# A graph-attention and mixture-of-experts kernel: where TensorE reads the addresses of a batch

## The chip, the cores and the metric

The kernel runs on one core of a Trainium2 chip. The metric is the device time of one launch, in microseconds (us), from the first to the last instruction of the program with what lies around them; lower is better. The engines of the core are named as in the profile: PE is TensorE's matmul, PEld its weight load, DVE is VectorE, ACT is ScalarE, POOL is GpSimd, SP is SyncE. A "q" behind a name (PEldq, ACTq) is the sequencer of that engine: the part that runs register and wait instructions and hands the others to the engine.

## The reference, cut to what matters

x has 6250 rows of 256, src and dst list 100000 edges sorted by dst.

```python
def _L0_gnn_ref(x, edge_index, W, attn, W_out):
    h = jnp.einsum('ni,hid->nhd', x, W)                  # 4 heads of 64
    e = jnp.einsum('ehd,hd->eh', h[src], a_src) + jnp.einsum('ehd,hd->eh', h[dst], a_dst)
    e = jnp.where(e > 0, e, 0.2 * e)
    alpha = jnp.exp(jnp.minimum(e - segment_max(e, dst)[dst], 20.0))
    alpha_norm = alpha / (segment_sum(alpha, dst)[dst] + 1e-08)
    return segment_sum(alpha_norm[:, :, None] * h[src], dst).reshape(N, 256) @ W_out

x = x + _L0_gnn_ref(_layernorm(x), edge_index, ...)
x = x + _L0_ffn_ref(_layernorm(x)[None], ...)[0]         # 8 experts, top 2, 256 -> 256 -> 256
```

## The kernel before, in words

A first part (lines 96 to 568) makes a table of h and its scores per node, and cuts the edges into tiles of 128, so that each tile's edges fall in one block of 125 destination nodes. The second part does everything else and is the part that the change touches. Its unit is a **batch** of 16 tiles; there are 52 batches.

**Iterations and slots.** Every engine has the same loop, `for it in range(-1, LAST)`, with 16 slots `k` in each iteration (lines 1282 to 1293 for TensorE). In iteration `it` TensorE sums the messages of batch `it`, one tile in each slot (`aggregate`, line 1113, 128x260 products into a PSUM bank), and works out the attention scores of batch `it + 1` in the same slots: the destination's part of the score of every edge (`d_of_edges`, line 1073, sixteen small products, called here D: eight in slot 0, D0, and eight in slot 1, D1), then the products of `chain` in slots 3, 5, 7 and 9 (lines 1081 to 1093), between which VectorE has its steps. VectorE starts on a batch's scores when D1 has ended (semaphore D), and line 1081 needs what VectorE makes of them (`eC`, line 794).

**The other stream.** From iteration 4 on the finished blocks of nodes go through the output projection, the layer norm, the router and the experts (`products`, lines 1137, 1183, 1189, 1214, 1240, 1249): three iterations for three blocks, 48 steps `s = s0 + k` with s0 = 0, 16 or 32 in turn. In slots whose s is in `FIRST = (0, 16, 25, 32)` these products stand ahead of the tile's aggregate, otherwise behind it; those of s = 18 stand in the slot of s = 17. With s0 = 0 slot 1 holds the second layer of an expert and the transposes of the router's weights (line 1240), with s0 = 16 it holds transposes and a first layer (lines 1189, 1137), with s0 = 32 a second layer (line 1183).

**Addresses.** Which PSUM bank a tile adds to, and which 12 columns of `d3` it reads, are data, and are kept in the table `tabs` (three buffers, one for each batch in flight, filled by SyncE's DMAs of line 691). TensorE reads them in groups of eight, by one TENSOR_LOAD on its sequencer (line 654). In front of each product with such an address stands a register instruction (FUSED_REGOPS in the trace, ISA in the program's order) that turns the number into an address; in `aggregate` it also waits for `zr`, ScalarE's word that the bank of the tile is cleared. A batch has four such groups: block numbers for D0 and for D1, read in `d_of_edges` right in front of their products, and banks for tiles 0 to 7 and 8 to 15, read by `bank_of_tiles` at the end of slot 15 of the iteration before and at the end of slot 7.

**ScalarE** (`evacuate`) copies a finished tile's sum out of its bank and clears the next bank, once a slot; **VectorE**'s `rescale` (line 841) has to scale the first bank of a batch before its tile 0 may be added (semaphore `rs`).

## Time and profile before

| | us |
|---|---|
| median of 3 runs | 1604.75 (1602.48 to 1605.58) |
| the profiled execution, its time | 1604.37 |
| its span, first to last instruction | 1602.6 |

| engine | busy us | share of the span |
|---|---|---|
| PE | 1447.0 | 90% |
| PEld | 1147.4 | 72% |
| DVE | 1098.8 | 69% |
| ACT | 981.0 | 61% |
| POOL | 829.2 | 52% |

The second part starts at about 94 us. Times in the rows are counted from the first instruction of the program.
### The profile page before, as it was taken

The page shows a single profiled execution, that of the slowest core. Times are in us where ns is not written, and L with a number is a line of the kernel's source. Part 1 is how long each engine was busy: PE and PEld are TensorE (multiplying, and loading weights), DVE is VectorE, ACT ScalarE, POOL GpSimd, SP SyncE. Part 2 cuts the span into 40 slices and gives each one's busy share as a digit, 9 for nine tenths or more (in the row PEclk, how much of TensorE's full clock was granted, in tenths as well). Part 3 has the DMA queues.
Part 4 walks back from the last instruction along what each step waited for, and adds up shares of the span by engine and source line. Part 5 has one row for each costly group of instructions (what it writes and reads, how often), then busy time and mean ns, then how long its engine had stood idle before and what let it go on. Part 6 is the DMA issues. An engine that isn't in the chain of part 4 may idle for free.

```text
span 1602.6 us, 29587 instructions
## 1 busy us (share of the span) xinstructions
PE 1447.0 (90%) x7327; PEld 1147.4 (72%) x7327; DVE 1098.8 (69%) x3031; ACT 981.0 (61%) x2505; POOL 829.2 (52%) x886
## 2 busy tenths in 40 slices
PE   5916776999999999999999999999999999999998
PEld 3813444777777777777777777777777878787887
DVE  6636665767777777767777777777776767677543
ACT  3705553666667575766666666666675767667632
POOL 1357777555555555555555555555564655551000
PEclk9966786899999999999999999999999999999999
DMA  9565644333343434343334334333334343464000
GB/s 220 141 189 141 179 134 132 102 104 109 106 116 96 118 100 114 105 116 105 114 103 110 109 108 112 109 109 100 117 102 119 96 124 92 123 91 63 1 17 17
DMA packets 89788, 174.83 MB, mean 109 GB/s; under 512 B 22455, under 2 KB 56049, under 8 KB 89593
## 3 DMA queue, kind: packets, MB, share of 16 engines
q0 software_dynamic: 40448, 111.89, 27.4%
q1 hardware_dynamic: 48071, 60.77, 12.7%
q8 instruction: 68, 1.11, 0.3%
q14 instruction: 95, 0.78, 0.2%
q10 hardware_dynamic: 1106, 0.27, 0.1%
HBM read 159.24 MB, written 14.43 MB: 108 GB/s over the span
## 4 chain that ended last, share of the span: by engine, by line
PE 72%; issue 8%; DVE 7%; ACT 4%; POOL 2%; ACTq 1%; DMA 0%; DVEq 0%; POOLq 0%
PE agg_ps L1113 23%; PE ob L1183 18%; PE hb L1137 15%; PE kbank L1073 4%; PE ob L1214 3%; POOL ring L740 2%; PE ob L1137 2%; PE ob L1249 2%; ACT acc L1326 2%; PE ob L1189 1%; DVE ring L848 1%; PE kbank L1089 1%; PE kbank L1081 1%; ACT agg_ps L1329 1%; ACT hT L1358 1%
## 5 line engine op out<-in xcount | busy, mean ns | idle before, releaser
L740 POOL DMA_INDIRECT ring<-table,srcE x832 | 796.9, 958 | 569.5 <-PE agg_ps L1113 330.4
L1113 PE MATMUL agg_ps<-ring,oh 128*128 128x260 f32 x1664 | 558.0, 427 | 27.8 <-ACT agg_ps L1329 16.3
L1326 ACT COPY acc<-agg_ps x831 | 307.8, 370 | 208.8 <-PE agg_ps L1113 151.9
L1183 PE MATMUL ob<-w_sb,hT 128*125 128x256 f32 x1600 | 408.9, 381 | 1.6
L1329 ACT COPY agg_ps<-zc 128x260 f32 x832 | 314.6, 378 | 98.6 <-ACT acc L1326 3.2
L1113 PEld LDWEIGHTS agg_ps<-ring,oh 128*128 128x128 f32 x1664 | 291.4, 199 | 94.4 <-issue 66.0
L1183 PEld LDWEIGHTS ob<-w_sb,hT 128*125 128x125 f32 x1600 | 296.4, 188 | 53.0 <-issue 9.6
L848 DVE TENSOR_TENSOR ring<-ring,kbank 128x1024 f32<-128x1024 f32 x208 | 244.8, 1214 | 50.2 <-ACT ring L1348 50.0
L1358 ACT ACTIVATE hT<-hb,b_sb 128x375 f32<-128x375 f32 (+1 forms) x272 | 154.0, 566 | 169.0 <-PE hb L1137 168.0
L785 DVE TENSOR_TENSOR oh<-kbank,relE 128x512 f32<-128x512 f32 x208 | 141.6, 681 | 126.5 <-PE kbank L1073 124.3
L983 DVE SCALAR_TENSOR_TENSOR y<-ob,cmb,y 125x256 f32<-125x256 f32 x400 | 188.9, 475 | 47.3 <-PE ob L1183 43.7
L1137 PE MATMUL hb<-xTh,w1l 128*128 128x376 f32 (+1 forms) x544 | 184.5, 420 | 2.6 <-ACT hT L1358 1.9
L1137 PE MATMUL hb<-xTh,w1h 128*128 128x376 f32 (+1 forms) x544 | 137.0, 333 | 0.0
L1137 PE MATMUL hb<-xTl,w1h 128*128 128x376 f32 (+1 forms) x544 | 136.6, 332 | 0.0
L1137 PEld LDWEIGHTS hb<-xTh,w1l 128*128 128x128 f32 x544 | 100.5, 191 | 23.6 <-ACT hT L1358 8.6
L1073 PEld LDWEIGHTS kbank<-d,OT 128*128 128x128 bf16 x832 | 67.1, 97 | 68.5 <-issue 53.7
L1073 PE MATMUL kbank<-d,OT 128*128 x832 | 83.1, 177 | 30.4 <-issue 26.0
L1137 PEld LDWEIGHTS hb<-xTl,w1h 128*128 128x128 f32 x544 | 98.0, 189 | 0.0
L1137 PEld LDWEIGHTS hb<-xTh,w1h 128*128 128x128 f32 x544 | 97.6, 190 | 0.0
L748 POOL TENSOR_TENSOR rstd<-mv,root_ 125x3 f32<-125x3 f32 (+1 forms) x17 | 14.8, 870 | 118.4 <-DVE mv L914 118.3
L1358 ACT ACT_TABLE_LOAD x50 | 64.2, 1283 | 1.3 <-issue 0.4
L485 PE MATMUL bank<-wcat,xnT 128*125 128x264 f32 x200 | 54.6, 396 | 5.4 <-DVEq L324 2.9
(271 smaller groups left out, 1376.7 us busy)
## 6 DMA issues: line engine op xcount, KB each, us to landing
OT<-relb_d SPq DMA_DIRECT2D x52, 512.0 KB
ring<-table,srcE POOLq DMA_INDIRECT x832
y<-in_x_dram SPq DMA_DIRECT2D x50, 125.0 KB
out_dram<-y SPq DMA_DIRECT2D x50, 125.0 KB
table<-hrow SPq DMA_DIRECT2D x25, 227.5 KB
acc<-in_x_dram SPq DMA_DIRECT2D x2, 1568.0 KB
acc<-in_L_ffn_w_dram SPq DMA_DIRECT2D x1, 2048.0 KB, 11.0
w_sb<-in_L_ffn_w_dram SPq DMA_DIRECT2D x1, 2048.0 KB
```

The lines of the kernel that those rows point to most:

```text
L485: m = T.matmul(bank[2 + b % 3][0:Q, 0:WIDE], xnT[:, b % 2, k, :], wcat[:, k, :], start=k == 0, stop=k == KC - 1)
L740: pool.indirect_dma_start(out=rings[b % RING][:, k, :], out_offset=None, in_=table[:, :], in_offset=bass.IndirectOffsetOnAxis(ap=srcE[:, t ...
L785: v.tensor_tensor(oh[:, (4 * b + q) % OHQ], iota_ps.unsqueeze(1).to_broadcast([P, 4, P]), relE[:, t0:t0 + 4].unsqueeze(2).to_broadcast([P, ...
L848: v.tensor_tensor(m, m, al.to_broadcast([P, 4, H, DH]), ALU.mult).then_inc(S["msg"], 1)
L983: v.scalar_tensor_tensor(y[0:Q, u, i, :], o[0:Q, 0:D], cmb[0:Q, u, i, e:e + 1], y[0:Q, u, i, :], ALU.mult, ALU.add).then_inc(S["ya"], 1)
L1073: m = T.matmul(D_ps[:, t * 3 * H:(t + 1) * 3 * H], OT[:, t * P:(t + 1) * P], d3[:, bass.ds(at[j], 3 * H)], start=True, stop=True)
L1113: T.matmul(aggf[:, bass.ds(half["at"][k % 8], ROW)], oh[:, (4 * b + q) % OHQ, k % 4, :], rings[b % RING][:, k, :], start=False, stop=True, ...
L1137: t = T.matmul(out_, a, b_, start=j == 0, stop=j == len(terms) - 1)
L1183: t = T.matmul(o[0:Q, 0:D], hT[:, e % 2, f, cols], w2_sb[:, e, f, :], start=f == 0, stop=f == KC - 1)
L1326: A.copy(accf[:, bass.ds(row_of[h][k % 8], ROW)], aggf[:, bass.ds(closed[h][k % 8], ROW)]).then_inc(S["ev"], 1)
L1329: A.copy(aggf[:, bass.ds(coming[h][k % 8], ROW)], zc[:, 0:1].to_broadcast([P, ROW])).then_inc(S["zr"], 1)
L1358: A.activation(hT[:, e % 2, f, 0:w], hbank[f][:, 0:w], ACT.Gelu, bias=b1_sb[:, e, f:f + 1]).then_inc(S["gl"], 1)
```

## The change

The four reads move. `d_of_edges` no longer reads its own addresses. A new function `blocks_of_tiles` reads the block numbers, at the end of slot 12 of the iteration before for D0 and at the end of slot 0 for D1, that is behind the products of D0 and in front of the aggregate of slot 1. `banks_of_tiles` reads the banks at the end of slot 14 of the iteration before (tiles 0 to 7) and at the end of slot 6 (tiles 8 to 15), one slot earlier than before. Each read waits for the batch's table (`fld`) itself. Nothing else moves, and the number of reads is the same.

```diff
+                    block_of, bank_of = {}, {}
+                    def blocks_of_tiles(b, half):
+                        pe.wait_ge(fld[b % RING], fetched(b))
+                        block_of[half] = loads(ENG.PE, tabs[0:1, b % 3, 2, 8 * half:8 * half + 8], (NB - 1) * 3 * H)
...
-                        at = loads(ENG.PE, tabs[0:1, b % 3, 2, 8 * half:8 * half + 8], (NB - 1) * 3 * H)
                         for j in range(8):
                             t = 8 * half + j
-                            m = T.matmul(D_ps[:, t * 3 * H:(t + 1) * 3 * H], OT[:, t * P:(t + 1) * P], d3[:, bass.ds(at[j], 3 * H)],
+                            m = T.matmul(D_ps[:, t * 3 * H:(t + 1) * 3 * H], OT[:, t * P:(t + 1) * P], d3[:, bass.ds(block_of[half][j], 3 * H)],
...
-                    def bank_of_tiles(b, h):
-                        if h == 0:
-                            pe.wait_ge(fld[b % RING], fetched(b))
-                        half["at"] = loads(ENG.PE, tabs[0:1, b % 3, 0, 8 * h:8 * h + 8], (AB - 1) * 512)
+                    def banks_of_tiles(b, h):
+                        pe.wait_ge(fld[b % RING], fetched(b))
+                        bank_of[h] = loads(ENG.PE, tabs[0:1, b % 3, 0, 8 * h:8 * h + 8], (AB - 1) * 512)
...
-                        T.matmul(aggf[:, bass.ds(half["at"][k % 8], ROW)], oh[:, (4 * b + q) % OHQ, k % 4, :], rings[b % RING][:, k, :],
+                        T.matmul(aggf[:, bass.ds(bank_of[k // 8][k % 8], ROW)], oh[:, (4 * b + q) % OHQ, k % 4, :], rings[b % RING][:, k, :],
...
                     def ahead(it, k):
                         if k in (0, 1) and it + 1 < NBAT:
                             d_of_edges(it + 1, k)
-                        if k % 8 == 7:
-                            b, h = (it, 1) if k == 7 else (it + 1, 0)
-                            if 0 <= b < NBAT:
-                                bank_of_tiles(b, h)
+                        if k == 0 and it + 1 < NBAT:
+                            blocks_of_tiles(it + 1, 1)
+                        elif k == 12 and it + 2 < NBAT:
+                            blocks_of_tiles(it + 2, 0)
+                        elif k == 6 and 0 <= it < NBAT:
+                            banks_of_tiles(it, 1)
+                        elif k == 14 and it + 1 < NBAT:
+                            banks_of_tiles(it + 1, 0)
...
+                    blocks_of_tiles(0, 0)
                     for it in range(-1, LAST):
```

TensorE's order at slots 0 and 1 of an iteration with s0 = 32, before (L1113 is the aggregate, L1073 are D0 and then D1, L1183 an expert's second layer, ISA the register instruction):

```order
L1113 MATMUL agg_ps<-ring0,oh 128x260
L654 TENSOR_LOAD tabs [waits e_msg,e_arg,e_oh,e_otc,e_fld1]
L1073 ISA
L1073 MATMUL kbank<-d3,OT 128x12
...
L1113 ISA [waits e_zr]
L1113 MATMUL agg_ps<-ring0,oh 128x260
L1183 MATMUL ob1<-w2_sb,hT 125x256 [waits e_ul,e_ya]
L1183 MATMUL ob1<-w2_sb,hT 125x256
L654 TENSOR_LOAD tabs
L1073 ISA
```

And the same place now (L1117 is the aggregate, L1079 are D0 and D1, L1192 the second layer):

```order
L1117 MATMUL agg_ps<-ring0,oh 128x260
L1079 ISA [waits e_msg,e_arg,e_oh,e_otc,e_fld1]
L1079 MATMUL kbank<-d3,OT 128x12
...
L654 TENSOR_LOAD tabs [waits e_fld1]
L1117 ISA [waits e_zr]
L1117 MATMUL agg_ps<-ring0,oh 128x260
L1192 MATMUL ob1<-w2_sb,hT 125x256 [waits e_ul,e_ya]
L1192 MATMUL ob1<-w2_sb,hT 125x256
L1079 ISA
```

The read in front of D0 has gone and one for D1 stands behind D0; D1 has no read in front of it any more.

TensorE's order from slot 12 to slot 0 of the next iteration, the same iteration, before (L1183, L1189 and L1137 are products of the other stream; ring2 is batch `it`, ring0 the next):

```order
L1183 MATMUL ob0<-w2_sb,hT 125x256
L1113 ISA [waits e_zr]
L1113 MATMUL agg_ps<-ring2,oh 128x260
...
L1137 MATMUL hb0<-xTh,w1h 128x376 x2
L1113 ISA [waits e_zr]
L1113 MATMUL agg_ps<-ring2,oh 128x260
...
L1189 MATMUL ob1<-ident,xn 128x125
L654 TENSOR_LOAD tabs [waits e_fld0]
L1137 MATMUL hb1<-xTh,w1l 128x376 [waits e_gl]
...
L1113 ISA [waits e_rs,e_zr,e_oh,e_msg]
```

And now:

```order
L1192 MATMUL ob0<-w2_sb,hT 125x256
L654 TENSOR_LOAD tabs [waits e_fld1]
L1117 ISA [waits e_zr]
...
L1146 MATMUL hb0<-xTh,w1h 128x376 x2
L654 TENSOR_LOAD tabs [waits e_fld0]
L1117 ISA [waits e_zr]
L1117 MATMUL agg_ps<-ring2,oh 128x260
...
L1198 MATMUL ob1<-ident,xn 128x125
L1146 MATMUL hb1<-xTh,w1l 128x376 [waits e_gl]
...
L1117 ISA [waits e_rs,e_zr,e_oh,e_msg]
```

One read now stands in front of tile 13's register instruction and one in front of tile 15's; the one between the products of slots 15 and 0 has gone.

## Rows read from the trace of the kernel before

**Rows 1.** The page: engine totals, and the chain that ended last.
```profile
PE 1447.0 (90%) x7327; PEld 1147.4 (72%) x7327; DVE 1098.8 (69%) x3031; ACT 981.0 (61%) x2505; POOL 829.2 (52%) x886
...
PE 72%; issue 8%; DVE 7%; ACT 4%; POOL 2%; ACTq 1%; DMA 0%; DVEq 0%; POOLq 0%
```
**Rows 2.** By line, L654 and L1073, whole span: ns min/median/max, first and last start.
```profile
L654 PEldq TENSOR_LOAD <-tabs x208: 585/591/1247, 95.0 to 1512.2; - x104
...
L1073 PEldq FUSED_REGOPS  x832: 37/37/42, 95.9 to 1479.6; - x167
```
**Rows 3.** Timeline of weight loads, iteration 28, s0 = 0: start, us, what.
```profile
870.11 0.30 PEld L1113 LDWEIGHTS agg_ps<-ring,oh 128*128 128x128 f32 x2 [0.60 <-issue]
871.26 0.94 PEld L1073 LDWEIGHTS kbank<-d,OT 128*128 128x128 bf16 x8 [0.85 <-issue]
872.22 0.30 PEld L1113 LDWEIGHTS agg_ps<-ring,oh 128*128 128x128 f32 x2
...
873.85 0.92 PEld L1073 LDWEIGHTS kbank<-d,OT 128*128 128x128 bf16 x8
...
876.46 0.11 PEld L1081 LDWEIGHTS kbank<-ident,eC 128*64 128x64 f32 x1 [0.26 <-DVE eC L794]
```
**Rows 4.** By line, L654, stretches at slots 0 and 1 of iteration 28.
```profile
L654 PEldq TENSOR_LOAD <-tabs x1: 604/604/604, 870.5 to 870.5; - x1
...
L654 PEldq TENSOR_LOAD <-tabs x1: 596/596/596, 873.1 to 873.1; - x1
```
**Rows 5.** Timeline of weight loads, iteration 29, s0 = 16.
```profile
903.06 0.27 PEld L1073 LDWEIGHTS kbank<-d,OT 128*128 128x128 bf16 x8 [0.15 <-issue]
```
**Rows 6.** Timeline of weight loads, iteration 30, s0 = 32.
```profile
925.46 0.30 PEld L1137 LDWEIGHTS hb<-xTh,w1l 128*128 128x128 f32 x2 [0.43 <-ACT hT L1358]
...
926.88 0.92 PEld L1073 LDWEIGHTS kbank<-d,OT 128*128 128x128 bf16 x8
...
929.01 0.61 PEld L1073 LDWEIGHTS kbank<-d,OT 128*128 128x128 bf16 x8
...
931.32 0.11 PEld L1081 LDWEIGHTS kbank<-ident,eC 128*64 128x64 f32 x1 [0.51 <-DVE eC L794]
```
**Rows 7.** Timeline of weight loads, iteration 4, before the other stream is dense.
```profile
214.62 0.91 PEld L1073 LDWEIGHTS kbank<-d,OT 128*128 128x128 bf16 x8 [0.80 <-issue]
...
216.32 1.04 PEld L1073 LDWEIGHTS kbank<-d,OT 128*128 128x128 bf16 x8 [0.39 <-issue]
...
219.06 0.13 PEld L1081 LDWEIGHTS kbank<-ident,eC 128*64 128x64 f32 x1 [1.19 <-DVE eC L794]
```
**Rows 8.** Timeline of weight loads, D1 of iterations 7, 49 and 48.
```profile
299.25 0.52 PEld L1073 LDWEIGHTS kbank<-d,OT 128*128 128x128 bf16 x8
...
1451.23 0.95 PEld L1073 LDWEIGHTS kbank<-d,OT 128*128 128x128 bf16 x8 [0.54 <-issue]
...
1424.42 0.49 PEld L1073 LDWEIGHTS kbank<-d,OT 128*128 128x128 bf16 x8
```
**Rows 9.** By line, L654, stretch at the end of iteration 29.
```profile
L654 PEldq TENSOR_LOAD <-tabs x1: 590/590/590, 924.8 to 924.8; - x1
```
**Rows 10.** Timeline of DVE: rescale before iteration 30, first step behind D1 of 28.
```profile
924.92 0.44 DVE L841 TENSOR_TENSOR agg_ps<-agg_ps,sc 128x260 f32 x1 [0.24 <-ACT agg_ps L1329]
...
874.89 0.69 DVE L785 TENSOR_TENSOR oh<-kbank,relE 128x512 f32<-128x512 f32 x1 [1.13 <-PE kbank L1073]
```
**Rows 11.** By line, L1113, register instructions of tiles 14 and 15; 12 and 13; 14 and 15.
```profile
L1113 PEldq FUSED_REGOPS  x2: 37/37/37, 865.1 to 867.8; - x2
...
L1113 PEldq FUSED_REGOPS  x2: 37/37/37, 918.4 to 919.5; - x2
...
L1113 PEldq FUSED_REGOPS  x2: 37/37/37, 210.2 to 211.0; - x2
```
**Rows 12.** Waits of ACT: who waited for whom, us, times, longest.
```profile
ACT hT L1358 <- PE hb L1137: 168.0, 120, 3.8
ACT acc L1326 <- PE agg_ps L1113: 151.9, 174, 4.8
```
**Rows 13.** By line, L778, the DVE's first use of the next table's batch, iteration 28.
```profile
L778 DVE TENSOR_SCALAR OT<-OT,pid x1: 741/741/741, 889.0 to 889.0; 128x2048 bf16<-128x2048 bf16 x1
```

More of the change, by code:

```diff
@@ L1093, in chain @@
                             T.transpose(rT_ps, rho[:, :], ident[0:ZW, 0:ZW]).then_inc(S["rT"], 1)
-                    half = {}
-                    def bank_of_tiles(b, h):
-                        if h == 0:
-                            pe.wait_ge(fld[b % RING], fetched(b))
-                        half["at"] = loads(ENG.PE, tabs[0:1, b % 3, 0, 8 * h:8 * h + 8], (AB - 1) * 512)
+                    def banks_of_tiles(b, h):
+                        pe.wait_ge(fld[b % RING], fetched(b))
+                        bank_of[h] = loads(ENG.PE, tabs[0:1, b % 3, 0, 8 * h:8 * h + 8], (AB - 1) * 512)
                     def aggregate(b, k):
```

## The prediction

> **What bounds the kernel now.** I read the page first, then the waits, then the timeline of weight loads in one iteration of each kind, with the sequencer's own instructions by line beside it. TensorE is busy for 90% of the span and holds 72% of the chain that ended last; 8% of that chain is "issue" [rows 1]. So TensorE sets the time, and part of it is not arithmetic but the sequencer that feeds it. The reader is to see two things. A read of eight addresses takes the sequencer 0.59 us, 208 times, and a register instruction takes 0.04 us [rows 2]. And the eight products of D come in two speeds. Where the sequencer hands them over one by one they take 0.92 us or more (0.12 each); where all eight were handed over while earlier products ran, they take 0.27 us [rows 3, 5].
>
> What stands behind D1 matters most. VectorE waits for it (1.13 us idle in iteration 28 [rows 10]), works, and lets line 1081 go. From the end of D1's loads to the load of line 1081 it is 876.46 - 874.77 = 1.69 us in iteration 28, 931.32 - 929.62 = 1.70 in iteration 30 and 219.06 - 217.36 = 1.70 in iteration 4, and each time TensorE stands idle before line 1081 [rows 3, 6, 7]. So the end of D1 is on the path in every kind of iteration, and a microsecond taken off there comes off the iteration, as long as what follows is paced by TensorE's own products.
>
> A read costs the sequencer its 0.59 us and a step of 0.05 behind it: 0.65 us. It costs time only where TensorE has nothing left in its queue.
>
> **The read in front of D0, and the new one behind D0.** In iteration 28 the aggregate's loads end at 870.41, the read starts at 870.5, and D0's loads start at 871.26, with a hole of 0.85 us [rows 3, 4]. This read goes, so D0 runs 0.65 earlier. But D0 is drained at the pace of the sequencer (0.94 us for eight [rows 3]), so at its end the queue is empty, and there the change puts the read for D1: 0.65 us, in front of the register instruction of tile 1. That one arrives when it did before, the aggregate of slot 1 starts at 872.22 as before, and nobody waits for D0 alone. **Net 0**, 51 times. This is the largest stall that the change seems to remove, and it only changes sides.
>
> **The read in front of D1.** It goes, with nothing in its place in slot 1. What that gives differs by kind of iteration:
> - s0 = 0 (15 iterations, 7 to 49). In iteration 28 the read starts at 873.1 and D1's loads take 0.92 us [rows 3, 4]. The products in front of them cover the read, but not the eight register instructions behind it. With those 0.65 us earlier, D1 is limited by TensorE: 0.27 us as in iteration 29 [rows 5]. Gain 0.92 - 0.27 = 0.65. The first of the kind has D1 in 0.52 (gain 0.25), the last has 0.95 behind a hole of 0.54, which gives the full 0.65 [rows 8]. I take 0.60: 15 x 0.60 = 9.0 us. VectorE can start that much earlier, since it was idle for 1.13 us [rows 10].
> - s0 = 16 (15 iterations). D1 takes 0.27 already [rows 5]. Gain 0.
> - s0 = 32 (14 iterations). D1 takes 0.61, and 0.49 in the last [rows 6, 8]. Gain 0.61 - 0.27 = 0.34: 14 x 0.34 = 4.8 us.
> - iterations 0 to 6. There is little or nothing in slot 1; D1 takes 1.04 behind a hole of 0.39 in iteration 4 [rows 7]. The gain is the whole 0.65, less in the iteration where transposes stand in between; 7 x 0.60 = 4.2 us.
>
> **The read at the end of slot 15.** It stands between the products of slots 15 and 0, and TensorE does run dry there: in front of iteration 30 the read starts at 924.8, and the product behind it is at 925.46 after a hole of 0.43 [rows 6, 9]. But tile 0 has to wait for VectorE's rescale, which ends at 925.36 [rows 10], and the read ends at 924.8 + 0.65, about 925.45. The sequencer gets about 0.1 us out of it there: 14 x 0.1 = 1.4 us. Bounds: nothing, where rescale decides, and the whole hole of 0.43 where that wait would shrink too (14 x 0.43 = 6 us). I take 0.1 because the end of rescale is a row. With s0 = 0 and 16 the rescale comes later than the read, and I count nothing.
>
> The Trainium skill ("Advanced Engine Details and Errata", Sequencer Loop) says that other engine instructions can be read and queued while the sequencer's own code runs. By that rule the plain product behind the read would not have waited, and the 1.4 us would not be there: the sum would be 18.0 instead of 19.4. The row speaks against it: the product comes 0.02 us behind the end of the read.
>
> **The new reads at the ends of slots 12, 14 and 6.** Each must find the sequencer waiting anyway. It does so for `zr`, since ScalarE clears a bank once a slot. In slot 14 to 15 the two register instructions are 2.7 us apart in the dense part and 0.8 in iteration 4; in slot 12 to 13 they are 1.1 apart [rows 11]. Less 0.12 for one's own step, 0.65 fits in each: in 0.98 and 2.6 with room, in 0.8 - 0.12 = 0.68 just so. Slot 6 has products waiting in the queue and a wait for `zr` of the same kind. Cost 0. If the cover is gone, a read costs up to 0.65 each time. The read at slot 12 needs the table of batch it + 2, which so far nobody on TensorE needed before slot 0. VectorE uses data of the same semaphore at 889.0 in iteration 28 [rows 13], ahead of TensorE's slot 13, and had no wait there worth a row. Cost 0. The read for batch 0 in front of the loop happens once; at most 0.65.
>
> **Sum.** 9.0 + 4.8 + 4.2 + 1.4 = 19.4 us. Against the profiled execution's time, 1604.37 - 19.4 = 1585.0; that execution is 0.4 under the median, so **1585.5 us** for a median. That the gain survives the rest of the iteration rests on who waits for whom: ScalarE waits for TensorE's first layers for 168 us in 120 places and for its aggregates for 152 us in 174 [rows 12], so its pace is hung on TensorE's and moves with it.
>
> **The rivals.**
> 1. *Part of the gain is swallowed at the end of the iteration.* From slot 12 on ScalarE's clearing paces the tiles [rows 11], and tile 0 waits for rescale. If ScalarE is there behind with work that does not hang on D1, half of what slot 1 gives is lost: 19.4 / 2, so 1595. For it: those waits. Against it: rows 12. Chance 0.17.
> 2. *Nothing moves.* The read was exchanged for one at the same spot, and the chain through ScalarE closes the iteration by itself: 1604. It would need ScalarE never to wait for TensorE between slot 1 and slot 12. Chance 0.07.
> 3. *More than the sum.* The hole before tile 0's products goes whole, and rescale, which hangs on ScalarE's last clearing, comes earlier with it: 6 us instead of 1.4, and a little in the iterations with s0 = 0, where a hole of that kind stands too: 1579. Chance 0.13.
> 4. *Slower.* At the end of slot 14 the sequencer reaches the read late, because it first has to hand over that slot's products, and the read then ends after `zr` has come. Tile 15, rescale and tile 0 are late by up to 0.65 us, 51 times: 33 us, less the 19.4: 1618. It decides from the point where less than 0.65 us is left of the wait; only iterations 1 to 4 are near it (0.68). Chance 0.04.
>
> By the skill's rule of before a read could not hold up a plain product at all, and rival 4 could only act through the register instruction. Its chance is set by the rows above.
>
> **How the numbers follow.** The forecast (1581 to 1590) has 0.59, then 0.17, 0.13, 0.07 and 0.04. From 1578 to 1597 lie the forecast, rival 1 and most of rival 3, which leaves less than 0.2 out. A difference under 0.2% (3.2 us) can't be told from none here. Faster: 0.59 + 0.17 + 0.13 = 0.89; same 0.07; slower 0.04.
>
> **What would show it.** In the profile after: D1 in 0.27 us in iterations with s0 = 0 and s0 = 32, still 1.70 us from there to line 1081; D0 without the hole of 0.85 in front, and instead a hole of about 0.65 between D0 and the aggregate of slot 1, which starts as long behind the aggregate of slot 0 as before (872.22 - 870.11 = 2.1 us); tiles 13 and 15 at their old distances (1.1 and 2.7 us). A group of three iterations shorter by 0.60 + 0.44, about 1.0 to 1.1 us. Wrong if the distance of tiles 14 and 15 grows, if line 1081 has no idle time before it although D1 is earlier, or if the distance of the two aggregates shrinks too, since then D0's read was worth something.

## The result, and the profile after

| | before | after |
|---|---|---|
| median | 1603.88 us (1602.48 to 1605.58, 6 runs) | 1600.03 us (1597.06 to 1665.54, 6 runs) |
| the profiled execution | 1604.37 | 1600.27 |
| its span | 1602.6 | 1598.4 |

The ratio is 0.997, interval 0.9959 to 0.9982: faster by 3.9 us, where 18 to 19 were forecast. One of the six executions with the change took 1665.54 us at a mean granted clock of 0.835, where the other five had 0.944 to 0.949, and the ratio is formed without it. The median lies 10 us above the forecast of 1581 to 1590, and 3 us above 1597, the upper end of the wider range.

From the page of the changed kernel, engine totals and the engines' shares of the chain that ended last (as [rows 1]):

```profile
PE 1429.7 (89%) x7327; PEld 1144.1 (72%) x7327; DVE 1098.9 (69%) x3031; ACT 980.5 (61%) x2505; POOL 827.7 (52%) x886
...
PE 64%; issue 11%; ACT 9%; DVE 5%; ACTq 3%; POOL 2%; DMA 0%; DVEq 0%; POOLq 0%
```

"issue" has more of the chain than before (11% for 8%), although the number of reads is the same. The slots show where TensorE waits for a read now. Weight loads of the changed kernel, iteration 28 (s0 = 0; as [rows 3]; L1117 is the aggregate, L1079 is D, L1087 the product behind VectorE's steps); columns are start, duration, what, and the idle time in front:

```profile
869.45 0.30 PEld L1117 LDWEIGHTS agg_ps<-ring,oh 128*128 128x128 f32 x2 [0.79 <-issue]
869.94 0.56 PEld L1079 LDWEIGHTS kbank<-d,OT 128*128 128x128 bf16 x5 [0.19 <-issue]
870.66 0.33 PEld L1079 LDWEIGHTS kbank<-d,OT 128*128 128x128 bf16 x3 [0.17 <-issue]
871.66 0.30 PEld L1117 LDWEIGHTS agg_ps<-ring,oh 128*128 128x128 f32 x2 [0.67 <-issue]
...
873.28 0.36 PEld L1079 LDWEIGHTS kbank<-d,OT 128*128 128x128 bf16 x8
...
875.35 0.11 PEld L1087 LDWEIGHTS kbank<-ident,eC 128*64 128x64 f32 x1 [0.35 <-DVE eC L794]
```

In this kind of iteration the mechanism is as forecast. The hole of 0.85 in front of D0 is 0.19, and one of 0.67 stands behind D0. D1's loads take 0.36 us instead of 0.92, and from their end to line 1087 it is 875.35 - 873.64 = 1.71 us, as before. VectorE waits 0.67 for them instead of 1.13:

```profile
873.77 0.69 DVE L785 TENSOR_TENSOR oh<-kbank,relE 128x512 f32<-128x512 f32 x1 [0.67 <-PE kbank L1079]
```

The end of D1 lies 873.64 - 869.45 = 4.19 us behind tile 0, and 874.77 - 870.11 = 4.66 in [rows 3]: 0.47 gained here, 0.54 in the median of the kind. Now iteration 30 (s0 = 32), after and, below it, the row of before that [rows 6] left out, the aggregate of slot 1:

```profile
924.87 0.36 PEld L1117 LDWEIGHTS agg_ps<-ring,oh 128*128 128x128 f32 x2
925.26 0.77 PEld L1079 LDWEIGHTS kbank<-d,OT 128*128 128x128 bf16 x8
926.70 0.30 PEld L1117 LDWEIGHTS agg_ps<-ring,oh 128*128 128x128 f32 x2 [0.68 <-issue]
...
927.90 0.46 PEld L1079 LDWEIGHTS kbank<-d,OT 128*128 128x128 bf16 x8
...
930.06 0.11 PEld L1087 LDWEIGHTS kbank<-ident,eC 128*64 128x64 f32 x1 [0.60 <-DVE eC L794]
```

```profile
926.43 0.36 PEld L1113 LDWEIGHTS agg_ps<-ring,oh 128*128 128x128 f32 x2
926.88 0.92 PEld L1073 LDWEIGHTS kbank<-d,OT 128*128 128x128 bf16 x8
927.82 0.30 PEld L1113 LDWEIGHTS agg_ps<-ring,oh 128*128 128x128 f32 x2
```

Before, D0 had no hole in front of it in this kind of iteration: products still in the queue covered the read. Its new place behind D0 has no cover. From tile 0 to tile 1 it is 926.70 - 924.87 = 1.83 us instead of 927.82 - 926.43 = 1.39. Here the exchange of sides cost 0.44 us.

How long an iteration takes is read best from windows laid from one tile 0 to the next. Iterations 28, 29 and 30, before and then after (window, its length, busy time and instructions of PE, PEld, DVE, ACT, POOL, then PE's granted clock, DMA share, GB/s):

```profile
870.11:899.18 29.07, 28.57 (x142) 22.67 (x143) 22.64 (x61) 18.41 (x46) 15.14 (x16) 1.00 0.42 121
899.18:926.42 27.24, 25.16 (x133) 20.15 (x132) 20.14 (x55) 18.31 (x46) 16.78 (x18) 1.00 0.36 102
926.42:951.97 25.55, 25.11 (x138) 20.66 (x137) 17.60 (x52) 17.29 (x44) 14.54 (x17) 1.00 0.36 104
```

```profile
869.46:898.06 28.60, 27.84 (x143) 22.17 (x144) 22.62 (x61) 18.39 (x46) 15.12 (x16) 1.00 0.42 123
898.06:924.88 26.82, 24.65 (x134) 20.07 (x133) 19.70 (x54) 18.02 (x46) 16.34 (x18) 1.00 0.37 101
924.88:950.69 25.81, 24.49 (x138) 20.35 (x138) 18.02 (x53) 17.55 (x45) 14.95 (x16) 1.00 0.37 105
```

These three gain 0.47, 0.42 and -0.26 us. Over iterations 8 to 49 the medians of those that ran wholly at full clock are 29.02, 27.30 and 25.61 before and 28.48, 26.84 and 25.81 after. I call their sum a **group**: 81.94 before, 81.14 after, 0.80 less, where 1.05 was forecast.

Not all iterations ran at full clock. Iteration 27 (s0 = 32 too), in it the stretch that ends with the router's products and the one behind it, and the same two stretches in 30:

```profile
842.15:869.46 27.31, 25.98 (x138) 21.43 (x138) 17.62 (x53) 17.56 (x45) 14.94 (x17) 0.94 0.36 100
...
845.55:849.80 4.25, 4.05 (x34) 3.47 (x30) 3.75 (x10) 1.63 (x5) 1.11 (x2) 1.00 0.52 169
849.80:853.30 3.50, 3.50 (x13) 2.78 (x13) 0.31 (x2) 0.46 (x1) 2.67 (x3) 0.53 0.41 114
```

```profile
928.30:932.50 4.20, 4.00 (x34) 3.42 (x30) 3.75 (x10) 1.62 (x5) 1.07 (x2) 1.00 0.49 165
932.50:936.00 3.50, 3.50 (x20) 2.94 (x21) 1.38 (x8) 1.22 (x3) 2.71 (x3) 1.00 0.46 119
```

In 27 a stretch of 3.4 us had the lower of TensorE's two clocks (1.2 GHz; a granted clock of 0.5), with 13 loads in it instead of 21, and the iteration took 27.31 instead of 25.81: 1.50 us. What TensorE did ahead of it is the same in 27 and in 30 (34 products and 30 loads each), and only 27 has the lower clock behind it. I call such a stretch a **fall**. In iterations 7 to 50 before has 2 and after has 5 (in its 15, 21, 27 and 33 at slot 4, in 42 at slot 10; before's in 9 at slot 4 and in 45 at slot 10).

The whole execution in stretches, before: ahead of the edge tiles (0 to 94 us), iterations 0 to 6, iterations 7 to 50.

```profile
0.00:94.00 94.00, 66.34 (x333) 51.88 (x333) 60.43 (x204) 49.23 (x159) 20.08 (x40) 0.98 0.74 177
...
123.73:295.51 171.78, 126.40 (x452) 80.83 (x452) 106.77 (x262) 92.82 (x263) 127.61 (x132) 0.70 0.50 141
295.51:1503.84 1208.33, 1160.27 (x6023) 932.66 (x6024) 882.31 (x2417) 800.27 (x2000) 658.44 (x691) 1.00 0.39 105
```

And after:

```profile
0.00:94.00 94.00, 69.48 (x333) 53.94 (x333) 59.40 (x203) 49.13 (x159) 18.11 (x38) 0.95 0.71 171
...
126.58:296.66 170.08, 126.15 (x452) 81.83 (x453) 107.15 (x262) 93.18 (x263) 126.91 (x132) 0.65 0.50 142
296.66:1499.70 1203.04, 1140.13 (x6023) 926.26 (x6024) 882.13 (x2417) 799.57 (x2000) 657.25 (x691) 0.99 0.39 105
```

Tile 0 of batch 0 comes at 126.58 instead of 123.73, 2.85 us later, behind code that is the same but for one read; iterations 0 to 6 take 1.70 less, 7 to 50 take 5.29 less. That makes -4.1 us, the difference of the spans (4.2).

### The profile page after: what moved, and what is told of

It is laid out like the page before. It is cut to its first block, busy times and chain, and to the rows that moved or that the text cites. A ratio compares the mean times of both kernels' runs of the same rounds, so it can differ in the third digit from the quotient of the medians.

```text
span 1598.4 us, 29587 instructions
## 1 busy us (share of the span) xinstructions
PE 1429.7 (89%) x7327; PEld 1144.1 (72%) x7327; DVE 1098.9 (69%) x3031; ACT 980.5 (61%) x2505; POOL 827.7 (52%) x886
## 4 chain that ended last, share of the span: by engine, by line
PE 64%; issue 11%; ACT 9%; DVE 5%; ACTq 3%; POOL 2%; DMA 0%; DVEq 0%; POOLq 0%
PE agg_ps L1117 21%; PE ob L1192 16%; PE hb L1146 13%; ACT acc L1336 4%; PE ob L1223 3%; ACT agg_ps L1339 2%; POOL ring L740 2%; PE ob L1146 2%; PE ob L1258 2%; PE kbank L1079 2%; ACTq L654 1%; ACT hT L1368 1%; PE ob L1198 1%; PE kbank L1087 1%; PE kbank L1095 1%
## 5 line engine op out<-in xcount | busy, mean ns | idle before, releaser
L1117 PE MATMUL agg_ps<-ring,oh 128*128 128x260 f32 x1664 | 565.9, 434 | 57.7 <-ACT agg_ps L1339 38.6
L1192 PE MATMUL ob<-w_sb,hT 128*125 128x256 f32 x1600 | 408.3, 380 | 1.6
L1117 PEld LDWEIGHTS agg_ps<-ring,oh 128*128 128x128 f32 x1664 | 296.3, 202 | 126.9 <-issue 98.7
L1192 PEld LDWEIGHTS ob<-w_sb,hT 128*125 128x125 f32 x1600 | 295.9, 188 | 52.9 <-issue 9.5
L1079 PEld LDWEIGHTS kbank<-d,OT 128*128 128x128 bf16 x832 | 55.3, 98 | 38.4 <-issue 23.4
L1079 PE MATMUL kbank<-d,OT 128*128 x832 | 63.3, 174 | 14.3 <-DVE OT L778 10.5
```

The source lines that it names most:

```text
L1079: m = T.matmul(D_ps[:, t * 3 * H:(t + 1) * 3 * H], OT[:, t * P:(t + 1) * P], d3[:, bass.ds(block_of[half][j], 3 * H)], start=True, stop=True)
L1117: T.matmul(aggf[:, bass.ds(bank_of[k // 8][k % 8], ROW)], oh[:, (4 * b + q) % OHQ, k % 4, :], rings[b % RING][:, k, :], start=False, stop= ...
L1192: t = T.matmul(o[0:Q, 0:D], hT[:, e % 2, f, cols], w2_sb[:, e, f, :], start=f == 0, stop=f == KC - 1)
```

## The experiments

Edits are given against the changed kernel. "Group" is the sum of medians above, "falls" are counted in the profiled execution, in iterations 7 to 50. Kernels that ran on one chip are compared with the runs of before on that chip.

### Each part alone, and the last read moved too

Four kernels on one chip, beside a before of 1604.16 us (1602.64 to 1607.25). **Only D0's read moved**; D1's is read in front of its products again, the banks at slots 7 and 15:

```diff
                         if k in (0, 1) and it + 1 < NBAT:
+                            if k == 1:
+                                blocks_of_tiles(it + 1, k)
                             d_of_edges(it + 1, k)
-                        if k == 0 and it + 1 < NBAT:
-                            blocks_of_tiles(it + 1, 1)
-                        elif k == 12 and it + 2 < NBAT:
+                        if k == 12 and it + 2 < NBAT:
                             blocks_of_tiles(it + 2, 0)
-                        elif k == 6 and 0 <= it < NBAT:
-                            banks_of_tiles(it, 1)
-                        elif k == 14 and it + 1 < NBAT:
-                            banks_of_tiles(it + 1, 0)
+                        if k % 8 == 7:
+                            b, h = (it, 1) if k == 7 else (it + 1, 0)
+                            if 0 <= b < NBAT:
+                                banks_of_tiles(b, h)
```

> Of the change only the read for D0 (slot 12 instead of in front of D0); the other three reads as in the kernel before. Theory X (the reads of slot 0 are on the path wherever the queue is empty there): iterations with s0 = 16 gain 0.65 us each in slot 0 (15 x 0.65 = 9.8), the early ones too (7 x 0.6 = 4.2), those with s0 = 0 nothing, since D1 there waits for VectorE's combine before line 1238, those with s0 = 32 next to nothing, since the read was covered by the six first-layer products in front of tile 0. Sum 14 us, so about 1590. Theory P (the prediction's: nobody waits for D0 alone): under 2 us.

Measured 1593.84 (1593.22 to 1596.20), ratio 0.9935 (0.9918 to 0.9952): 10.3 us faster than before, and better than the whole change. Group 80.80 (29.03, 26.73, 25.03), 6 falls. Iteration 28:

```profile
862.90 0.30 PEld L1117 LDWEIGHTS agg_ps<-ring,oh 128*128 128x128 f32 x2 [0.59 <-issue]
863.38 0.96 PEld L1079 LDWEIGHTS kbank<-d,OT 128*128 128x128 bf16 x8 [0.19 <-issue]
864.36 0.30 PEld L1117 LDWEIGHTS agg_ps<-ring,oh 128*128 128x128 f32 x2
...
866.59 0.97 PEld L1079 LDWEIGHTS kbank<-d,OT 128*128 128x128 bf16 x8 [0.56 <-issue]
```

Tile 1 comes 1.46 us behind tile 0 (2.11 in [rows 3]). With s0 = 0 this is lost again, since D1 with its read ends at 867.56, 4.66 behind tile 0 as before. With s0 = 16 and 32 about 0.6 is kept in each (27.30 to 26.73 and 25.61 to 25.03). So D0's read was on the path in these two kinds. Theory X had the direction, and s0 = 32 wrong: it expected next to nothing there.

**Only D1's read moved** (behind D0), the edit the mirror of the one above: D0's is read in front of its products, none at slot 12.

> Of the change only the read for D1 (behind D0 instead of in front of D1); the other three as before. Theory X: the read behind D0 is never covered, so it costs 0.65 us in slot 0 of every iteration; it gives back 0.65 in D1 with s0 = 0 (net about 0) and in the early ones (net 0), nothing with s0 = 16 (15 x 0.65 = 9.8 lost) and 0.2 to 0.35 with s0 = 32 (14 x 0.35 = 5 lost). Sum 15 us slower, about 1619. Theory P: the read in front of D0 remains, so the same 0.65 comes on top, but only its gain at D1 was counted: 15 to 18 us faster.

Measured 1628.06, ratio 1.0142 (1.0125 to 1.0159): 24 us slower. Group 82.80 (28.98, 27.78, 26.03), 9 falls. With both reads around D0, tile 1 is 0.5 later with s0 = 16, 0.6 with s0 = 32. The group explains 0.86 x 14.7 = 13 of the 24 us; 7 falls more than before at 1.5 are about 10. 15 us were expected by theory X.

**Only the banks moved** (slots 6 and 14), both block reads where they were.

> Of the change only the two bank reads (slots 6 and 14 instead of 7 and 15). Theory X: the products of slot 0 with s0 = 32 start 0.35 us earlier and tile 0 too, but D0's read there is then less covered, so 0.1 to 0.35 is left: 14 x 0.2 = 3 us faster. Theory P: 1.4 us faster. Both say within noise; the trace tells by the distance from tile 15 to tile 0 and to D0 in those iterations.

Measured 1601.61, ratio 0.9982 (0.9971 to 0.9994). Group 81.56 (29.03, 26.69, 25.84), 3 falls, all with s0 = 0. With s0 = 16 the next tile 0 comes 0.6 sooner, and 0.23 of it is given back with s0 = 32: 0.38 us per group, 5.6 in all by this kind of sum, 2.6 by the time (expected 3 and 1.4). With s0 = 32 tile 1 is 1.72 us behind tile 0 in the median, where before has 1.46: tile 0 moved, and D0's read in front of D0 holds tile 1 back.

**D1's read at slot 13** of the iteration before, so that slots 0 and 1 hold no read:

```diff
-                        if k == 0 and it + 1 < NBAT:
-                            blocks_of_tiles(it + 1, 1)
+                        if k == 13 and it + 2 < NBAT:
+                            blocks_of_tiles(it + 2, 1)
...
                     blocks_of_tiles(0, 0)
+                    blocks_of_tiles(0, 1)
```

> The changed kernel with one more move: the read for D1 stands at the end of slot 13 of the iteration before instead of behind D0, so that no read is left in slots 0 and 1. Theory X: the hole of 0.55 to 0.65 us between D0 and tile 1 goes in every iteration: 15 x 0.65 with s0 = 16, 14 x 0.6 with s0 = 32, 7 x 0.6 early, and 0.3 to 0.4 with s0 = 0 where combine limits: 28 us under the changed kernel, about 1572. Theory P (tile 1 is not what the iteration waits for, only D1's end is, and that is limited by TensorE's products): under 5 us. If the granted clock falls less often, up to 8 us more.

Measured 1581.75 (1576.26 to 1585.34), ratio 0.9843 (0.9818 to 0.9869): 22 us faster than before, 18 faster than the change (28 by theory X, under 5 by theory P). Group 79.88 (28.40, 26.50, 24.97), 2.06 less than before's, 7 falls. Iteration 28 has neither hole:

```profile
859.41 0.30 PEld L1117 LDWEIGHTS agg_ps<-ring,oh 128*128 128x128 f32 x2 [0.81 <-issue]
859.90 0.96 PEld L1079 LDWEIGHTS kbank<-d,OT 128*128 128x128 bf16 x8 [0.19 <-issue]
860.88 0.30 PEld L1117 LDWEIGHTS agg_ps<-ring,oh 128*128 128x128 f32 x2
...
862.56 0.88 PEld L1079 LDWEIGHTS kbank<-d,OT 128*128 128x128 bf16 x8
```

But D1 takes 0.88 again: with TensorE sooner there, the sequencer's eight register instructions pace it. Its end is 863.44 - 859.41 = 4.03 behind tile 0 (4.19 with the change). The price stands at tile 14, which with s0 = 16 comes 0.41 later behind the read at slot 13.

### Further places, on a second chip

The next kernels ran where before takes 1731.36 us (1719.84 to 1738.82). **Before again:**

> The kernel before, unchanged, profiled once more. Theory X: the start of tile 0 of batch 0 (134.3 us in the first profile of before, 137.0 after the change, with the same code in front of it) and the number of short half-speed stretches differ between executions of one program: tile 0 between 134 and 138. Theory P: tile 0 comes at 134.3 again, and the 2.7 us are the change's.

Profiled at 1733.99. Tile 0 of batch 0 comes at 142.33 us. (The 134.3 and 137.0 of the expectation count from 10.5 us ahead of the first instruction; they are the 123.73 and 126.58 of above.) With a first part that is slower as a whole on this chip, that answers neither theory; the executions on the first chip do, further below. VectorE waits here for a gather, a wait that the first profile of before does not have ("remote" is the gathered rows' arrival):

```profile
DVE oh L785 <- remote: 52.3, 6, 27.2
```

Group 87.4, 13 falls. So there are waits here that the first chip did not show, and the small differences have to be read with care.

**Two products of 256 columns in front of each router's products**, written over by the router (behind tile 3's aggregate, s0 = 32; the expectations call the place slot 4). Where falls begin there, TensorE has just run D1's products of 12 columns, an expert's second layer, and the router's products of 8 columns:

```diff
                             u = g % 2
+                            for _ in range(2):
+                                T.matmul(ob1[0:Q, 0:D], xTh[:, u, 0, 0:Q], w1h[:, 0, 0, :], start=True, stop=True)
```

> The changed kernel with two more products of 256 columns in front of each router (line 1137 by its place, 128x8 products, slot 4 with s0 = 32), written over by the router; 0.2 us of TensorE each time, 17 times, so 3.6 us of added work. Theory X (TensorE's granted clock falls behind the stretch with D1, a hole and the router, all of few columns): the half-speed stretches in iterations with s0 = 32, five after the change, go to none or one, each worth 1.5 us; net 1597 against 1600. Theory R (the falls have nothing to do with what TensorE does there): still about five, 1603.

Measured 1738.45, ratio 1.0039 (1.0008 to 1.0070). One fall in slots 3 to 5 of the 14 iterations with s0 = 32 (before has 3 on this chip, with no such products), 13 in all, and 7 us slower than before. Again on a third chip, beside the change:

> The changed kernel with two products of 256 columns in front of each router's eight-column products (slot 4 of the iterations with s0 = 32); what they write is written over by the router. Theory (the stretches at 1.2 GHz that follow slots 1 to 4 of these iterations come from too few columns streamed there): fewer than 2 of 14 such iterations fall to 1.2 GHz behind slot 4, where the change has 5; each fall is worth 1.5 us and the added products cost 0.22 us each time (3 us), so 1 to 5 us faster than the change. Rival (the falls have nothing to do with the columns): as many falls as the change, and 3 us slower.

Measured 1742.10, ratio 1.0018 (1.0002 to 1.0034), 6 of 14 in those slots (the change: 6), 15 in all (the change: 10), and 12 us slower than the change, where the products were taken for 3. So one and the same kernel has 1 of 14 in one profiled execution and 6 of 14 in another: a count of one execution says little by itself. Two products do not remove the falls.

**D1's read at slot 10, the banks' at 8** instead of 14, and the same with the products of s = 19 ahead of the aggregate:

```diff
-                        if k == 0 and it + 1 < NBAT:
-                            blocks_of_tiles(it + 1, 1)
+                        if k == 10 and it + 2 < NBAT:
+                            blocks_of_tiles(it + 2, 1)
...
-                        elif k == 14 and it + 1 < NBAT:
+                        elif k == 8 and it + 1 < NBAT:
...
-                    FIRST = (0, 16, 25, 32)
+                    FIRST = (0, 16, 19, 25, 32)
```

> All four reads where the sequencer waits longest: D1's at the end of slot 10, D0's at 12, banks at 8 and 6. Against the version with D1's read at slot 13 (1581.8) the 0.4 us that slot 14 loses with s0 = 16 come back: an undisturbed group of three iterations 79.5 instead of 79.9 us, 1575 to 1578. Rival: slot 14 waits for VectorE's norm and POOL's root, not for the read, and nothing changes: 1582.

> The version before with the other stream's products of step 19 in front of line 1081 instead of behind (slot 3, s0 = 16), where TensorE stands idle for 1.4 us. Theory X: the hole is real time, and the four passes of a second layer (0.86 us) fill it: 15 x 0.8 = 12 us faster, 1563 to 1567. Rival: the products wait themselves (VectorE's accumulate is behind its score work in its own order), so they hold up line 1081: no gain or up to 10 us slower.

Measured 1736.93, ratio 1.0028 (0.9994 to 1.0063), 24 falls; and with the last line 1730.72, ratio 0.9996 (0.9969 to 1.0023), 16 falls. No gain on this chip. The last line is worth 6 us of the 12 expected, which lies within the two intervals. How they would do on the first chip is not known, so they say nothing on the price of the read at slot 13.

### The change and D1 at slot 13 again

On a third chip, where before takes 1739.77 us (1733.12 to 1745.52).

> The change itself, unaltered, beside its variants on one chip. Theory (clock and slots): where the gathered rows arrive as in the profile of before, a group of three undisturbed iterations is 80.9 to 81.4 us (81.94 before), of which part is taken back by stretches at 1.2 GHz; median 3 to 9 us below before (0.995 to 0.998). Rival (the first part of the first profile of before happened to be 2.7 us early, and the change is worth more than it seemed): 0.991 to 0.994.

The change: 1730.49, ratio 0.9950 (0.9930 to 0.9970), 10 falls. The ratio is as the theory had it, the group (86.57) is not.

> The changed kernel with D1's read at the end of slot 13 of the iteration before, so that no read is left between D0 and tile 1. Theory: the hole of 0.55 us behind D0 was on the path, and the earlier result (0.984) repeats where the gathered rows arrive in time: ratio to before 0.982 to 0.987, 17 to 24 us faster than the change itself in the same set. Rival (that result was the luck of one chip): within 0.3% of the change itself.

D1 at slot 13: 1751.66, ratio 1.0059 (1.0030 to 1.0089). What was 22 us faster on one chip is 12 us slower here. The group says otherwise (85.44, the change 86.57), though it rests on 2 undisturbed iterations with s0 = 32. There are 23 falls, in 22 of the 44 iterations: 12 of 14 with s0 = 32, 8 of 15 with s0 = 16.

> D1's read at slot 13, and the two products of 256 columns in front of each router. Theory (columns): with 7 falls of 1.5 us in the earlier run without them, 5 to 7 of these go, less 3 us for the added products: 3 to 7 us faster than D1's read at slot 13 alone. Rival (falls do not depend on the columns there): 3 us slower than it.

With the two products of 256 columns: 1750.42, ratio 1.0055 (1.0038 to 1.0072), 21 falls, 6 of 14 in slots 3 to 5 of s0 = 32 where it had 11. Within what can be told, no difference.

### Eight products, or half a router

Once more the change and D1 at slot 13, on the chip with the same number as in the section above, but now with before at 1730.34 us (1720.54 to 1738.11), 9 us less than there:

> The change itself once more, beside the two experiments on the router. Theory (what the slots show, less stretches at 1.2 GHz): 0.995 to 0.998 of before, as in the two results so far. Rival: the next chip gives more than 0.9% or nothing.

> The changed kernel with D1's read at the end of slot 13 of the iteration before. It gave 0.984 on a chip with a before of 1604 us and 1.006 on one with 1740 us, where 22 of 44 iterations held a stretch at 1.2 GHz instead of 7. Theory (the undisturbed iterations are shorter on every chip; the sum hangs on those stretches): a group of three undisturbed iterations is 1.5 us or more shorter than before's wherever it runs; if before takes about 1605 us the ratio is 0.982 to 0.988, if it takes about 1735 us it is 1.002 to 1.009. Rival (the two results were chance): the ratio does not go with before's time.

The change 1724.16, ratio 0.9964 (0.9930 to 0.9997), group 85.65, 16 falls. D1 at slot 13 1741.16, ratio 1.0061 (1.0021 to 1.0101), group 86.04, 19 falls. The ratio is again over 1 where before is slow, as expected, and the change again faster than before; D1 at slot 13's group is 1.4 us under the 87.4 of the before profiled on the other slow chip, less than the 1.5 I had put down.

**Eight products of 256 columns** at the router (`range(8)` in the edit above), and **half of the router's products** left out:

```diff
-                                t = exact(ob1[0:Q, i * NE:(i + 1) * NE], [(xTh[:, u, k, cols], xTl[:, u, k, cols]) for k in range(KC)],
-                                          [(rwh[:, k, :], rwl[:, k, :]) for k in range(KC)])
+                                t = exact(ob1[0:Q, i * NE:(i + 1) * NE], [(xTh[:, u, k, cols], xTl[:, u, k, cols]) for k in range(1)],
+                                          [(rwh[:, k, :], rwl[:, k, :]) for k in range(1)])
```

> The changed kernel with eight products of 256 columns in front of each router's eight-column products (slot 4 of s0 = 32), about 1.7 us each time; the router writes over what they give. With two such products the stretches at 1.2 GHz behind slot 4 did not go. Theory (a lack of columns there, two products being too few): at most one of 14 such iterations falls to 1.2 GHz in slots 3 to 5. Rival (the columns of that place do not matter): 4 to 8 of 14, as with the change itself. Time by both: 15 to 24 us slower than the change, since the products cost 14 x 1.7 us.

> The changed kernel with half of the router's products (one of the two halves of its sum is left out, so that the experts chosen differ; the amount of work behind does not). Nine weight loads and eight-column products less, 1.0 us, in slot 3 of s0 = 32. Theory (these products are the stretch of few columns that lets the clock fall): 0 to 2 of 14 iterations fall in slots 3 to 5, so 14 x 1.0 + 3 x 1.5 = 18 us faster than the change or more. Rival (the router has nothing to do with it): 4 to 8 of 14 fall, and 10 to 14 us faster.

Both leave **no** fall in slots 3 to 5 of s0 = 32, in 14 iterations each, where the change has 5 in the same set, 6 in the one before and 4 in its first profile. Eight products: 1730.53, ratio 0.9993 (0.9974 to 1.0011), 6 us slower than the change and not the 15 to 24 expected, 5 falls in all. Half a router: 1706.74, 17 us faster than the change (18 or more by the theory, 10 to 14 by the rival), 9 falls in all. Iterations 7 to 50 of the change, of eight products and of half a router, one window each:

```profile
354.19:1632.20 1278.01, 1162.24 (x6023) 933.12 (x6024) 884.36 (x2417) 802.78 (x2000) 664.22 (x691) 0.97 0.37 99
```

```profile
357.71:1626.89 1269.18, 1158.89 (x6134) 934.80 (x6135) 882.21 (x2417) 800.18 (x2000) 668.81 (x691) 0.99 0.37 100
```

```profile
352.63:1605.82 1253.19, 1138.94 (x5897) 912.89 (x5898) 882.51 (x2417) 801.51 (x2000) 658.61 (x691) 0.99 0.38 101
```

With 112 products more, this part took 8.8 us less in the profiled executions. That is not a gain: the profiled execution of the change (1732.75) was 8.6 us over its own median, and by the medians the eight products are 6 us slower. Over all executions the mean granted clock is 0.925 in the median with the change, 0.930 with the eight products and 0.928 with half a router. So the falls behind slot 3 seem to go with what TensorE does in that slot. The router's products alone do not bring them on: before has them too and 1 fall there in 14 in its first profile, and the kernel with only the banks moved has none. Where the 14 x 1.5 us of the eight products went has two answers that these rows don't part: falls that went, and cover at the end of such an iteration (tile 4 is 1.2 us later, the next tile 0 hardly at all).

### The eight products in before and with D1 at slot 13

On a further chip, before at 1740.80 us:

> The kernel before with eight products of 256 columns in front of each router's products, as the changed kernel had them in cols_8 (the router writes over what they give). With them the changed kernel had no stretch at 1.2 GHz in slots 3 to 5 of s0 = 32, and took 0.9993 of before. Theory (with the clock level there, the change is worth what the undisturbed iterations show, 0.8 to 1.7 us per group of three, 12 to 25 us): before_cols_8 takes 1.006 to 1.014 of before, and its 0 to 1 falls in those slots show that the added columns work here too. Rival (the clock took nothing back): 1.002 to 1.004, the same distance to cols_8 as from before to the change (0.995 to 0.997).

> D1's read at slot 13, with the same eight products in front of each router. Without them it took 1.006 of before on chips with a before of 1730 to 1740 us, where 12 and 7 of 14 iterations with s0 = 32 and 8 and 5 of 15 with s0 = 16 held a stretch at 1.2 GHz. Theory (those stretches take its gain back): the ones in slots 3 to 5 of s0 = 32 go (0 to 2 left), those of s0 = 16 stay; the ratio to before is 0.999 to 1.004 although 14 x 1.5 us of products are added, that is 4 to 12 us under d1_at_13's. Rival: 1.5 us x 14 slower than without them, 1.015 to 1.018.

Before with them: 1750.43, ratio 1.0055 (1.0036 to 1.0075), no fall in slots 3 to 5 of s0 = 32, 9 in all. The changed kernel had 0.9993, so they are 0.62% apart, plus or minus 0.26 by their intervals, against 0.36 to 0.50% without the products. It lies under the 1.006 of the one theory and over the 1.004 of the other: this doesn't tell whether the change is worth more at level clock. With D1 at slot 13: 1756.84, ratio 1.0101 (1.0075 to 1.0127), between both expectations as well; 2 falls left in slots 3 to 5 of s0 = 32, 9 of 15 iterations with s0 = 16 still have one. Beside before with the same products it is 6 us slower.

## Why the prediction was wrong

The largest miss that the experiments tie to a step is the sum for the iterations with s0 = 32. Each was to gain 0.34 us at D1 and 0.1 at the read of slot 15, with D0's read at net 0. The undisturbed ones became 0.20 us longer (25.61 to 25.81), and the gain at slot 15, which was more than 0.1, shows in those with s0 = 16, whose windows end at that tile 0. A term for the clock was left out of the sum altogether. The distances below are medians over the undisturbed iterations from 8 to 49.

**"Net 0", 51 times, for D0's read: wrong with s0 = 32.** The step took the hole of 0.85 of iteration 28 for every kind. [rows 6] showed D0 with no idle time in front of it in iteration 30, which said that the read was covered there. Behind D0 it is not: tile 1 comes 0.44 us later behind tile 0 in iteration 30, 0.40 in the median (1.86 for 1.46). With the banks alone it is 1.72, so by that comparison 0.26 of the 0.40 comes of tile 0 being early and 0.14 of the exchange. With s0 = 0 and 16 tile 1 came when it did before, as forecast (2.09 for 2.07).

**D1 with s0 = 32: 0.14 us instead of 0.34.** Its loads take 0.47 us (0.61 before), not the 0.27 that was taken over from s0 = 16, and their end lies 1.66 behind tile 1 instead of 1.80. That is 2.0 us of the 4.8.

**The read at the end of slot 15: 0.1 was too little, and the reason was wrong.** Tile 0 of s0 = 32 comes 2.49 us behind tile 15 instead of 2.95: 0.46 earlier. I had held rescale's end for the limit. But rescale ended at 925.36 [rows 10] and tile 0 started at 926.43, 1.07 us later. Between them stand the six loads of slot 0's first layer, which wait for the read and not for rescale (in TensorE's order only tile 0's register instruction, behind them, waits for `rs`), so the whole hole in front of them was to be had. After the change rescale ends as long behind tile 15 as before (1.88 us) and still 0.61 ahead of tile 0:

```profile
923.83 0.43 DVE L841 TENSOR_TENSOR agg_ps<-agg_ps,sc 128x260 f32 x1 [0.24 <-ACT agg_ps L1339]
```

```profile
923.91 0.30 PEld L1146 LDWEIGHTS hb<-xTh,w1l 128*128 128x128 f32 x2
924.19 0.36 PEld L1146 LDWEIGHTS hb<-xTl,w1h 128*128 128x128 f32 x2
924.53 0.36 PEld L1146 LDWEIGHTS hb<-xTh,w1h 128*128 128x128 f32 x2
924.87 0.36 PEld L1117 LDWEIGHTS agg_ps<-ring,oh 128*128 128x128 f32 x2
```

Rival 3 had the hole going whole, though not by this way. The late tile 1 eats most of it: together the kinds 16 and 32 gain 0.26 us (0.46 less 0.20) instead of 0.44.

**D1 with s0 = 0: right, a little too large.** 0.54 instead of 0.60, since D1's eight loads take 0.36 to 0.37 and not 0.27.

So a group gained 0.80 instead of 1.05, and 14.7 groups 11.7 us instead of 15.2 (9.0 + 4.8 + 1.4). Medians flatter the gain: by the means of the same iterations (28.86, 27.46 and 25.72 before, 28.34, 27.12 and 25.94 after) iterations 7 to 50 gained 9.3 us, falls counted apart: 7.4 with s0 = 0, where 9.0 were forecast, and 1.9 with the other two kinds together, where 6.2 were.

**Iterations 0 to 6: 1.7 us instead of 4.2.** In iteration 4 the end of D1 lies 219.20 - 215.80 = 3.40 behind tile 0 after, and 217.36 - 213.53 = 3.83 before: 0.43 of the 0.60:

```profile
215.80 0.50 PEld L1117 LDWEIGHTS agg_ps<-ring,oh 128*128 128x128 f32 x2 [2.07 <-issue]
...
218.89 0.31 PEld L1079 LDWEIGHTS kbank<-d,OT 128*128 128x128 bf16 x7 [0.28 <-issue]
```

Over the seven it is 0.35, 0.41, 0.32, 0.27, 0.43, 0.00 and 0.19, 2.0 us together, and the part took 1.7 less. It also ran at a lower granted clock, 0.65 instead of 0.70 in the rows above; no experiment tells how much of the miss is the clock's.

**The cost of the clock was no term of the sum.** Before has 2 falls in iterations 7 to 50 and the change has 5; by what the iterations that hold them are longer than the mean of their kind, 2.9 and 6.9 us, so 4.0 more. Three more may be too many for a typical execution: the profiled one of the change has the lowest mean granted clock of its five (0.944 of 0.944 to 0.949), that of before one of the highest (0.955, where before on the first chip of the experiments has 0.947 to 0.956, 0.952 in the median). Falls at slot 4 go with what TensorE does ahead of them: eight products more and half a router left none there, in one profile each (the eight also in before, and 2 of 11 or 7 with D1 at slot 13). That the change itself causes its three more is not shown: on the slower chips its mean clock is not lower than before's (0.925 and 0.922 in one set).

**Ahead of tile 0: 2.85 us.** The execution of before ran its first 94 us at a clock of 0.98, that of the change at 0.95. In the four kernels on the first chip tile 0 came at 124.3 to 127.1 us with the same code ahead of it but for a read. A scatter that a sum against one profiled execution can't see.

The account: 19.4 forecast; less 5.9 in the slots (15.2 - 9.3), 2.5 in iterations 0 to 6, 4.0 for falls and 2.85 ahead of tile 0 leaves 4.15. Measured in the profiles 4.1. It closes because it counts out two executions; only its first term is tied to the change by experiments.

**The reads at slots 6, 12 and 14 cost nothing**, as forecast. Rival 4 did not come about: with the banks alone there was a gain, and tiles 13 and 15 kept their distances (in the medians of all kinds within 0.1 us). Rival 2's time was nearly right by luck, and its reason wrong: D1's end did move line 1087, with the same 1.7 us between them. Rival 1 named no loss that was found.

**What was missed as a possibility:** D0's read was worth about 0.6 us in two of three kinds once nothing took its place (10 us, by D0's read alone), and my own sentence, that it "only changes sides", was the reason to ask for a third side. D1's read at slot 13 gives it: 1581.75 us, faster than both kernels on the first chip. In the two later sets, where before takes 1740 and 1730 us, it is slower than both, so no version here is better everywhere; the change itself was faster than before in all three.

What makes D1 at slot 13 slow there isn't settled. It has more falls than the change (23 for 10, 19 for 16), and within one kernel the executions with a lower clock were the longer ones: over nine of D1 at slot 13 beside the before of 1730.34, the time rises by 1.5 us for each 0.001 of mean clock lost. By that slope, and by the medians of the mean clock (0.915 for 0.925, 0.913 for 0.925), the lower clock would be worth 14 us in the one set and 18 in the other, of the 21 and 17 us by which it is slower than the change. That is an estimate from what goes together, and no experiment parts cause and effect: with all but two of its falls in slots 3 to 5 of s0 = 32 taken away (the eight products) its loss did not become a gain.

## What to carry to other kernels

A stall that appears in front of a group of instructions in one iteration has to be looked for in each kind of iteration before it is multiplied, also where a row shows no idle time: cover that is there in one kind and not in the new place turns "net 0" into a cost. If a step is exchanged for one of the same price on the other side, first try the place where neither stands. Before a wait is taken for a limit, look whether the engine has other work between the end of that wait and the instruction. And where a trace shows stretches at the lower clock, compare several executions, on more than one chip, before a small difference is explained: between the two profiles here they were worth as much as the change.

## What the runs showed of the hardware

- A read of eight addresses behind D0's last load left TensorE without a load for 0.66 to 0.69 us in 49 of the 51 iterations of the changed kernel; in before, with no read there, it is 0.01 to 0.04.
- A stretch of 3.4 us at 1.2 GHz cost 1.5 us in the five iterations of the changed kernel that have one (27.30 to 27.40 for 25.81). In other kernels it cost less or more: 0.85 to 0.98 us in three iterations with s0 = 0 (banks alone), 2.2 in one with s0 = 32 (D1 at slot 13). Ahead of those at slot 4 TensorE had run D1 (12 columns each), an expert's second layer, waited for VectorE, and run the router's products, 8 columns each, 18 in 2.1 us:

```profile
L1146 PE MATMUL ob<-rwh,xTl 128*125 128x8 f32 x6 | 1.2, 268 | 0.0
...
L1146 PEld LDWEIGHTS ob<-rwh,xTl 128*125 128x125 f32 x6 | 1.0, 188 | 0.1
```

TensorE counts as busy for 4.05 of 4.25 us between 845.55 and 849.80, and the clock was at 1.2 GHz from 850.0 on; in iteration 30 it counts for 4.00 of 4.20, and the clock stayed at 2.4. With 8 x 256 columns more, no fall followed in 14 iterations of the change and 14 of before, nor in 14 of the change with half of these products less; with 2 x 256 more, 1 of 14 followed in one profile and 6 in another.

- The same kernel took 1604 us on the chip of the first experiments and 1730 to 1741 on three others (on one of them 1740 in one set and 1730 in the next), and a variant's sign changed between them (0.984 and 1.006). The profiles of the slower ones show waits for gathered rows. What is behind it stays open.
